# Side work in a new order in all stages, and 256 and 384 slots instead of 320 and 320 in every expert

## The reference, cut to what matters

```python
x = x + attn(cond(x, cond_8))                       # rotary attention, 2 heads of 128
y = cond2(x, cond_8)                                # silu(x Wu) * (x Wg) Wd, expert = argmax(cond_8)
logits = y @ Wg.T
top_v, top_i = top_k(logits, 2); gates = softmax(top_v)
pos = cumsum(onehot(flat_e)) - 1                    # place of a token in its expert's list
keep = pos < cap                                    # cap = 640
h = exp_batches @ W1; h = gelu(h[:, :512]) * h[:, 512:]
out = segment_sum(where(keep, gates, 0) * (h @ W2)[flat_e, pos])
x = x + out
out = sum_e w_e * mlp_e(x) + mlp_shared(x)          # gelu(x G) * (x U) D; w is 0 but for 2 of 8
x = x + scan(sigmoid(out Wg + bg), tanh(out Wc + bc))
z = x W_base + lora(x); x = x + gelu(z ternary(W1) + b1) ternary(W2) + b2
```

## Time and profile before

| | us |
|---|---|
| median of 3 runs | 993.82 (991.86 to 994.32) |
| profiled execution | 994.64, span 993.4 |
| PE busy | 948.7 (96%), 4918 matmuls |
| DVE busy | 520.9 (52%) |
| ACT busy | 445.7 (45%) |
| POOL busy | 278.9 (28%) |

### The profile page before, as it was taken

The page is one execution under the profiler, slowest core; times in us unless marked ns, Lnnn a source line. Parts: engine busy times, 40 slices in busy tenths (PEclk is TensorE's granted clock), DMA queues, the critical chain, the costliest instruction groups (busy, mean ns, idle before and its releaser), DMA issues.

```text
span 993.4 us, 13248 instructions
## 1 busy us (share of the span) xinstructions
PE 948.7 (96%) x4918; PEld 781.0 (79%) x4918; DVE 520.9 (52%) x964; ACT 445.7 (45%) x831; POOL 278.9 (28%) x251
## 2 busy tenths in 40 slices
PE   5989999999999999989998999999999999998998
PEld 2667867777779999989776888888888888876786
DVE  5745453466646655577467433333333333688544
ACT  2555565423155444555344334244343342325775
POOL 1333221402066575464351024032040230100000
PEclk9999999999999999999999999999999999999999
DMA  7130001202325434432521301103003002000011
GB/s 265 42 109 22 22 1 64 75 22 85 107 54 129 135 115 132 165 101 75 176 58 32 127 1 48 80 1 127 1 1 127 0 22 106 1 1 0 1 43 43
DMA packets 22449, 67.49 MB, mean 68 GB/s; under 512 B 4770, under 2 KB 12210, under 8 KB 19570
## 3 DMA queue, kind: packets, MB, share of 16 engines
q1 hardware_dynamic: 16658, 39.89, 11.4%
q0 software_dynamic: 5440, 26.50, 8.9%
q10 hardware_dynamic: 288, 0.26, 0.1%
HBM read 55.09 MB, written 9.45 MB: 65 GB/s over the span
## 4 chain that ended last, share of the span: by engine, by line
PE 76%; DVE 11%; ACT 5%; issue 4%; DMA 2%; SPq 1%; POOL 0%; another core or an unknown queue 0%; ACTq 0%; DVEq 0%; POOLq 0%
PE banks L1008 16%; PE banks L1010 15%; PE banks L1009 15%; PE banks L1240 4%; PE banks L1241 4%; PE banks L1239 4%; PE banks L1098 3%; PE banks L1082 2%; PE banks L1289 2%; PE banks L1288 2%; PE banks L1275 1%; PE banks L1276 1%; PE banks L1089 1%; DVE state L1961 1%; PE banks L1166 1%
## 5 line engine op out<-in xcount | busy, mean ns | idle before, releaser
L1008 PE MATMUL banks<-input_hi,mlp_hi 128*128 128x512 f32 x376 | 150.0, 399 | 0.0
L1010 PE MATMUL banks<-input_hi,mlp_lo 128*128 128x512 f32 x376 | 149.4, 397 | 0.0
L1009 PE MATMUL banks<-input_lo,mlp_hi 128*128 128x512 f32 x376 | 148.8, 396 | 0.0
L1506 ACT CAST hidden_hi<-hidden 128x512 fp32r<-128x512 f32 x96 | 59.6, 621 | 177.5 <-DVE hidden L1902 107.0
L2098 POOL TENSOR_TENSOR mlp_lo<-weight_stage,mlp_hi 128x768 fp32r<-128x768 f32 x32 | 58.9, 1842 | 219.4 <-ACT mlp_hi L1480 219.4
L1908 DVE TENSOR_TENSOR hidden_lo<-hidden,hidden_hi 128x512 fp32r<-128x512 f32 x96 | 66.5, 693 | 71.1 <-ACT hidden_hi L1506 70.4
L1902 DVE SCALAR_TENSOR_TENSOR hidden<-banks,L_expert_weight,gelu 128x512 f32<-128x512 f32 x64 | 48.1, 751 | 99.2 <-PE banks L1010 96.0
L2058 POOL TENSOR_TENSOR ffn_w_lo<-weight_stage,ffn_w_hi 128x512 fp32r<-128x512 f32 x48 | 62.0, 1296 | 88.1 <-ACT ffn_w_hi L1439 87.8
L1008 PE MATMUL banks<-expert_in_hi,ffn_w_hi 128*128 128x320 f32 x256 | 81.1, 317 | 5.7 <-DVE hidden L1834 5.4
L1500 ACT ACTIVATE gelu<-banks 128x512 f32<-128x512 f32 x96 | 57.6, 600 | 62.5 <-PE banks L1010 62.4
L1010 PEld LDWEIGHTS banks<-input_hi,mlp_lo 128*128 128x128 f32 x376 | 70.7, 188 | 16.6
(11 more groups left out here) (332 smaller groups left out, 2153.1 us busy)
## 6 DMA issues: line engine op xcount, KB each, us to landing
weight_stage<-in_packF SPq DMA_DIRECT2D x8, 1536.0 KB, 7.2
weight_stage<-in_shared SPq DMA_DIRECT2D x2, 3072.0 KB, 10.2
expert_output<-y_rows SPq DMA_DIRECT2D x40, 128.0 KB
weight_stage<-in_cond_w SPq DMA_DIRECT2D x4, 512.0 KB, 6.2
residual<-in_xT SPq DMA_DIRECT2D x4, 512.0 KB, 11.0
first_half_swapped<-first_half SPq DMA_DIRECT2D x32, 64.0 KB, 2.0
routed_input<-x_rows SPq DMA_DIRECT2D x16, 128.0 KB, 1.8
weight_stage<-in_ffn_w SPq DMA_DIRECT2D x2, 1024.0 KB, 7.7
```

The source lines that it names most:

```text
L1008: pe.matmul(o, wh, dh, start=(i == 0), stop=False)
L1009: pe.matmul(o, wh, dl, start=False, stop=False)
L1010: last = pe.matmul(o, wl, dh, start=False, stop=(i == len(terms) - 1))
L1506: act.copy(hiD[n % 4][:, :], prod_t[n % 2][:, :]).then_inc(done)
```

## The change

It has these parts.

1. **Widths.** `half_of` and `width_of` give the slots of a half: 256 and 384 in every expert, before 320 and 320. The first half then needs two turned tiles, before three.
2. **Spins.** 34 in all instead of 77: none ahead of the logits (5 each) and of the slots (16), 6 instead of 12 ahead of the first scores, 16 and 4 instead of 13, 4 and 4 at the first rows.
3. **POOL's waits.** Each `wf_lo`, and `wm_lo` of the first MLP, is put on the list by `pool_in_turn` and waits also for the last signalled DVE unit before it in DVE's list.
4. **MLP pieces.** Pieces 0 and 1 of the first MLP are split on DVE instead of on POOL.
5. **Attention.** In the chunks with short scores three banks serve scores and three the output, before four and two; one of the later inputs is taken earlier. The last output product is interleaved with the first ups.
6. **First FFN and routing.** `all_chunks` is written out: the routing of a chunk stands between the ups of the next; the last chunk's `lgT` comes after two downs, and its `at` before its rows 1 to 3.
7. **Last gate.** Its transpose moves from the start of expert 1 into expert 2.
8. **Combining.** In steps 1 to 7 of the first MLP as before; the tiles left come in the odd steps of the second, where before they came in the other steps of the first.
9. **Tail.** The sums of magnitudes come first among the tail's weights and start in step 3 of the last MLP; `adapted` has its own banks and is woven into the first chunk of the feed-forward.
10. **Transfers.** The projection weights are issued before the third part of the conditioning weights instead of before the fourth; a rope swap is two transfers of 64 alternate partitions (128 KB) instead of four of 32 (64 KB), with the host's rows in another order.

```diff
+def half_of(e, h):
+    end = 2 * P
+    return slice(end, CAP) if h else slice(0, end)
...
-DVE_PIECES = (5, 7)
+DVE_PIECES = (0, 1, 5, 7)
...
-SPIN = {"first scores": 12, "logits": 5, "slots": 16, "first rows": 13, "next rows": 4, "first hidden": 4}
+SPIN = {"first scores": 6, "first rows": 16, "next rows": 4, "first hidden": 4}
...
+    def pool_in_turn(*unit):
+        pool.append(unit)
+        lets_go[unit] = next(u for u in reversed(dve) if u[0] not in UNSIGNALLED)
...
-        use("score", [(0, 1), (2, 3)] if long else [(0,), (1,), (2,), (3,)])
-        use("out", [(6,), (7,)])
+        use("score", [(0, 1), (2, 3)] if long else [(0,), (1,), (2,)])
+        use("out", [(6,), (7,)] if long else [(6,), (7,), (3,)])
...
-    run(weave(attention(1), chain(some(fold, 2), later_input(2), fold, rotated("k", 2), later_input(3), rotated("q", 2), value_tiles(2))))
+    run(weave(attention(1), chain(some(fold, 2), later_input(2), fold, later_input(3), rotated("k", 2), rotated("q", 2), value_tiles(2))))
...
+            if between:
+                next(between, None)
             dve.append(("hid_lo", c, i))
...
-                pool.append(("wf_lo", e, 2 * k + part))
+                pool_in_turn("wf_lo", e, 2 * k + part)
...
+    def routed_behind_first(c):
+        two_largest(c)
+        yield
+        product("turn2", "cnt", c)
+        places(c)
+        yield
+        dve.append(("digits", c))
+        yield
...
+        for c in range(2, NCH):
+            between = routed_behind_first(c - 1)
+            yield from up_units(c, 0, 2, between)
+            if c == 2:
+                dve.append(("at", 0))
+            yield from up_units(c, 2, HT, between)
             if c == NCH - 1:
                 use("down", [(3,), (4,), (5,), (0,), (1,), (2,)])
-            yield from logits(c)
-            yield from behind
-        yield from down_chunk(NCH - 1)
-
-    weights = chain([None] * 4, split0(1), [None] * DELAY, split_expert(0))
+            for t in range(QT - 2):
+                down(c - 1, t)
+                if c == 2 and t == 0:
+                    inverse(0)
+                yield
+            rows_of(c - 1, 0)
+            dve.append(("at", c - 1))
+            if c < NCH - 1:
+                down(c - 1, 2)
+                yield
+            logits(c)
+            yield
+            rows_of(c - 1, 1, 2)
+            if c == NCH - 1:
+                down(c - 1, 2)
+                yield
+            else:
+                down(c - 1, 3)
+                rows_of(c - 1, 3)
+            product("turn2", "lg", c)
+            dve.append(("first", c))
...
+        last = NCH - 1
+        two_largest(last)
+        down(last - 1, 3)
+        rows_of(last - 1, 3)
+        yield
+        down(last, 0)
+        yield
+        product("turn2", "cnt", last)
+        places(last)
+        dve.append(("digits", last))
+        rows_of(last, 0)
+        dve.append(("at", last))
+        rows_of(last, 1, 2, 3)
+        for s in ("gap", "pick1_sub", "back_rows"):
+            dve.append((s,))
+        for t in range(1, QT):
+            down(last, t)
+            yield
+        inverse(last - 1)
+        inverse(last)
...
-            yield from turn_in(0, FIRST_HALF, ST)
+            yield from turn_in(0, 2, ST)
         yield from split_expert(e)
+        if e == 2:
+            product("turn3", "last_gate")
+            dve.append(("last_gate_in",))
+            yield
...
-            if e == 1:
-                product("turn3", "last_gate")
-                dve.append(("last_gate_in",))
...
     def tail_weights():
-        yield
+        for n in range(2):
+            for q in range(4):
+                dve.append(("abs", n, q))
+                yield
         for b in range(B):
             dve.append(("lbw", b))
+            product("work", "total", b)
+            dve.append(("scale", b))
...
+            if n + 1 == 3 * B and u > 2:
+                next(following, None)
...
-            if u > (6 if n + 1 < 3 * B else 2):
+            if u > 6 if n + 1 < 3 * B else u > 3 and u % 2:
...
-            if n or u:
+            if 0 < u < IT1 if n == 0 else u % 2:
...
+            product("adapted", "ad", c, m)
...
+    for i in range(FT):
+        if i in (0, 3, 6):
+            adapted(i // 3 + 1)
+        ffn_unit(0, i)
     for c in range(1, NCH):
-        adapted(c)
-    for c in range(NCH):
-        ffn_chunk(c)
+        for i in range(FT):
...
-                    pe.wait_ge(*ready("xe_lo", e, ST - 1 if h else FIRST_HALF - 1))
+                    pe.wait_ge(*ready("xe_lo", e, -(-hs.stop // P) - 1))
...
-                pe.wait_ge(*ready("he_lo", e, 0 if (j + 1) * P <= HALF else 1, IT - 1))
+                pe.wait_ge(*ready("he_lo", e, 0 if (j + 1) * P <= half_of(e, 0).stop else 1, IT - 1))
...
+                if n == 0 and q == 0:
+                    dve.wait_ge(*ready("dn", 4, CPB * IT1 - 1))
+                    dve.wait_ge(ld["tail"], 16 * (len(TAIL) - 1))
+                    dve.wait_ge(ld["tail_gru"], 16)
...
+                pool.wait_ge(*ready(*lets_go[unit]))
...
-            if i == 3:
+            if i == 2:
...
-            for a in range(4):
-                to, at = slice(a * HR, (a + 1) * HR), (a ^ 1) * HR
-                sp.dma_start(swap_t[n % 2][to, :], same_t[n % 2][at:at + HR, :]).then_inc(ld[f"swap{n % 2}"], 16)
+            for a in range(2):
+                sp.dma_start(swap_t[n % 2][a:P:2, :], same_t[n % 2][1 - a:P:2, :]).then_inc(ld[f"swap{n % 2}"], 16)
```

183 lines of the change are left out of this document (83 added, 100 removed).

## The result

The changed kernel took 976.06 us in the median (974.89 to 976.67, 4 runs), the kernel before 994.07 in the same comparison: a ratio of 0.982, with a 95% interval of 0.9801 to 0.9839. The profiled execution has a span of 974.6 us against 993.4, 18.8 less. The forecast was 968, with a range of 957 to 981; the time lies in the range, 8 us above the forecast. It does not lie in the forecast case (961 to 975, chance 0.62) but in the next one, 975 to 985, to which the prediction gave 0.20.

A forecast was written before the change was run, and what follows sets the result against it. TensorE (PE), busy 948.7 of 993.4 us, was taken as the bound, with idle PE and spin matmuls to win. Terms summed to 25.4 us off the profiled 994.64, so 969.2, and 968 for the median; range 957 to 981.

The forecast's parts named there:

- forecast case: Whole kernel: the summed terms come about as told, with two rivals inside the band; 961 to 975 us, chance 0.62.
- Start: Before the first scores: earlier projection weights and a rope swap of fewer transfers gain 2.6 us (0 to 4).
- Attention to expert 0: Terms for attention (4.0), first FFN and its routing (4.5), end of the routing (3.0) and expert 0's tiles (2.1).
- third and fourth term: Before expert 0: end of the routing gains 3.0 us (1.5 to 6), expert 0's first product on two tiles 2.1.
- The two bounds named against the routing's end: POOL subtractions of 1.3 us meet DVE's short routing steps; the first gather may wait for a store of rows.
- Expert 0's two tiles: Start of expert 0: its first product waits for two turned tiles instead of three, gaining 2.1 us.
- Burst: Expert 6: pieces on DVE and POOL's waits prevent back-to-back subtractions that hold `hidden_lo`; gain 4.5 us (0 to 5).
- The new waits: Experts: POOL's subtractions start later, so DVE lags PE; cost 3.5 us (0 to 7), mostly at the third down product.
- the lag is bigger than I have it: Rival, experts: the new waits cost 1.3 us an expert, giving 974.5 us; inside the forecast case, no own chance.
- half comes back: Rival: half of the 19.3 us from attention, first FFN, routing, MLP and tail returns; 978, band 975 to 985, chance 0.20.
- signs of being wrong: `hidden_lo` means over 1 us, PE waiting for `xe` or `w1` in every expert, a gather awaiting a store, unchanged tail waits.
- tail: Around the scans at the end: earlier sums of magnitudes and own banks for adapted products gain 4.0 us (1 to 6).

The follow-up runs named there:

- n_spin: nowait with 12 spin matmuls ahead of the last chunk's count, in idle time of PE: 959.70 us, ratio 0.9699.
- before_pieces: The kernel before with only MLP pieces 0 and 1 split on DVE instead of POOL: 986.03 us, ratio 0.9936.
- n_w320: nowait with halves of 320 and 320 in every expert, expert 0 waiting for three turned tiles: 964.94 us, ratio 0.9720.
- n_pieces57: nowait with MLP pieces 0 and 1 back on POOL: 969.24 us, ratio 0.9794.
- n_gate4: nowait with POOL's gathers of the last expert's gates beside expert 4 instead of expert 3: 963.45 us, ratio 0.9737.
- nowait: The changed kernel without POOL's new waits in experts 1 to 7; expert 0 keeps them: 966.83 us, ratio 0.9724.
- fetch_late: The changed kernel with the 1.5 MB fetch of expert 2's weights issued after the last stores of rows: 975.75 us, ratio 0.9808.

## Why the prediction was right in its range and 8 us low

**Start (2.6, measured 1.5).** The weights came as told and PE began 1.1 earlier, of which 0.8 was left when its spins began (31.11, before 31.90). The swap's second half gave 0.7 instead of 1.4. These are POOL's products of the keys and the queries, DVE's `times_sin` of the queries, and PE's first scores:

```profile
29.84 1.78 POOL L2085 TENSOR_TENSOR keys<-times_cos,times_sin 64x512 f32<-64x512 f32 x1 [26.07 <-DVE times_sin L1723]
32.32 1.77 POOL L2085 TENSOR_TENSOR queries<-times_cos,times_sin 64x512 f32<-64x512 f32 x1 [0.70 <-DVE times_sin L1723]
...
30.51 1.66 DVE L1723 TENSOR_TENSOR times_sin<-first_half_swapped,rope_sin 128x512 f32<-128x512 f32 x1
...
34.44 0.46 PE L1146 MATMUL banks<-keys,queries 128*128 128x128 f32 x2 [1.86 <-POOL queries L2085]
```

The swap was there early, and so `times_sin` began at 30.51, under POOL's keys, 29.84 to 31.62. It took 1.66 instead of 0.7, and the queries followed at 32.32. I had named POOL's keys as what lies in the way, but only through POOL's own queue, not through DVE.

**Attention to expert 0 (13.6, measured 13.9).** The sum is right, its parts are not, and that they meet is luck. Up to the last up product 13.6 us are won, where attention and first FFN have 8.5: 4.7 of them before the first up (term 4.0) and 8.9 from the first up to the last (term 4.5, with the last output product). A part of the 8.9 is the clock: in the kernel before the granted clock was 0.73 in 192 to 196 and 0.84 in 196 to 200, behind small products of the router, in the changed kernel 1.00; the prediction did not see it. From the last up product to the last down product 0.7 is lost, and from there to expert 0 1.0 won, where the third and fourth term have 5.1 together. The two bounds named against the routing's end both came in: DVE's `column_hit` and `token_at_column` of chunk 2 took 1.59 and 1.44 us under three of POOL's subtractions, where those of the last chunk take 0.48 and 0.49, and the gather waited for a store. That the store would queue behind the fetch of 1.5 MB was not in the working, nor was the clock, which fell after the 2.7 us for `routed_bf` and again after the 3.2 for the gather. Expert 0's two tiles, told at 2.1, gave 1.1, for the spins and turns between them ran at the low clock (0.72 in 260 to 264); in n_spin, at full clock, they gave 2.1.

**Burst (4.5).** Too small, 5.9 in before_pieces' expert 6, and wrong in what does it. The wait of 4.1 is gone as told. But the 0.4 for the restart were too little, for in the kernel before the clock falls behind that wait:

```profile
436.00:440.00 4.00, 4.00 (x20) 3.95 (x19) 2.91 (x6) 2.61 (x7) 2.24 (x2) 0.57 0.01 2
```

At half for 3.4 us, PE does 1.7 us of work less. "Each subtraction waits for the DVE step before it, so no burst can form" was one cause too many.

**The new waits (-3.5, range -7 to 0).** This is the step that failed: the stage is 10.1 us longer with them (204.64 against 194.56), beyond my end of 7, and the waits of expert 0 and of the MLP pieces aren't in that. I had the DVE step at 2.15 for 256 columns; it is 2.06. For 384 columns I had only PE's time of 2.1 a step (12 x 0.175) and took it that DVE keeps up; its step is 2.31. So the lag grows in the first two steps of the second half, where POOL is still at work. And I priced one late wait at the third down product. In the trace PE also stops at steps of both halves, some five times in expert 1, once in expert 2, mostly for less than 0.25 us, then 0.3 to 0.6 at the third down product, for `y_rows` behind the last steps. Experts 1, 3 and 6 lose 2 to 3 us each, expert 3 in part by the clock. The rival "the lag is bigger than I have it", 974.5, is what came. The case in whose band the time fell, "half comes back", is not: the shaved waits of attention, first FFN, MLP and tail did not come back. Of the signs of being wrong that the prediction names, two came, if not in every word: `hidden_lo` over 1 us beside POOL (1.24 in the median, 0.99 in the mean of all 64), and a gather that waits for a store.

**Widths (-0.5) and last gate (0.9).** The widths alone make no difference that n_w320 shows. The last gate's wait is gone, but before_pieces, which has the gate in its old place, doesn't have it either, so that the move removed it isn't shown.

**First MLP (3.8, measured 4.1) and tail (4.0, measured 5.6).** The mechanism was right in both.

**The rule against the trace.** Whether DVE can be passed over by several subtractions is shown twice more: 8.09 us under six of them in n_pieces57 and 4.09 under three in n_gate4, and none over 1.3 in the changed kernel, where they can't come in a row. By the Trainium skill, page "SBUF — State Buffer", section "Who interferes with whom", the one that starts first has the shared ports for its whole instruction; of a second instruction of the same engine, which gets them again ahead of the one that waits, it says nothing, and that is what decides here.

## What to carry to other kernels

When two engines disturb each other, a wait that puts the one behind the other isn't free: ask which part of the other's step it may lie beside at no cost, and release it there. Against a burst, look first for what makes the engine late; here two pieces of work moved to another engine removed it without a wait. A stall of a few us on PE costs more than its length where the clock falls behind it, so look at the granted clock of the window after it. And a transfer that is off the path still sets the time of the small one issued behind it, on whichever side of it you put it.

## What the runs showed of the hardware

A DVE step with two operands in SBUF that waits for POOL isn't served after POOL's running instruction, if the next is ready: 3.0 us under two in n_spin, 4.09 under three in n_gate4, 5.68 under five in the kernel before, 8.09 under six in n_pieces57. PE's granted clock was at half for about 3.4 us in the changed kernel and in nowait after 2.7 us of idle time, and for longer in fetch_late after the same; 12 matmuls that compute nothing, 2.76 us, kept it at full in n_spin. In the kernel before it also fell behind small products of the router, with PE not idle. Where it was low, products of 256 columns took 0.21 us instead of 0.12. Five small gathers by POOL, 1.25 us apart, made its subtractions late, so that two or three came in a row; in nowait they went with an idle DVE instead, whose cause is open.
